# Two mixture layers with their routing rows broadcast by way of memory, in a transformer stack on one core

## The reference

```python
# layer 5, last part (8 experts): one expert per token
h = layernorm(x + attn_out, ln1_g, ln1_b)
_, top_i = top_k(softmax(h @ router_w.T + router_b), 2)
assign = max(top_i)                      # one expert number a token
for e in range(8):
    oe = gelu(h @ w1[e].T + b1[e]) @ w2[e].T + b2[e]
    out = where(assign == e, oe, out)
x += layernorm(h + out, ln2_g, ln2_b)
# layer 7 (16 experts, 4 chosen out of 2 of 4 groups, and a shared one)
scores = sigmoid(x @ gate_w.T);  s = scores + gate_bias   # s picks, scores weigh
comb[token, idx] = scores[token, idx]
y = einsum('tei,edi,te->td', silu(x @ w1) * (x @ w3), w2, comb)
z = silu(x @ ws1.T) * (x @ ws3.T) @ ws2.T
x += y + z
```

## Time and profile before

| | us |
|---|---|
| median of 3 runs (lowest, highest) | 1003.81 (1001.76, 1006.44) |
| the profiled execution, its own time | 1007.03 |
| its span on the core | 1005.2 |
| PE busy in the span | 730.2 |
| DVE busy in the span | 590.4 |
| ACT busy in the span | 355.2 |

### The profile page before, as it was taken

One profiled execution on the slowest core, in us unless ns is written; L12 is line 12 of the kernel. 1 busy time (PEld: TensorE's weight loads), 2 busy tenths in 40 slices (PEclk: granted clock), 3 DMA queues, 4 the chain that ended last, 5 costly groups with the idle time before them and its releaser, 6 DMA issues. The chain is left out here.

```text
span 1005.2 us, 13391 instructions
## 1 busy us (share of the span) xinstructions
PE 730.2 (73%) x3910; PEld 465.9 (46%) x3910; DVE 590.4 (59%) x2022; ACT 355.2 (35%) x634; POOL 251.8 (25%) x304
## 2 busy tenths in 40 slices
PE   2677762849839775588575757869886688699998
PEld 1233322848838621234364545556654233245554
DVE  6666644326305453775534564979887666576773
ACT  5355420624415332533332311212332466433231
POOL 2240466440343262512423321230210110000000
PEclk9999775869959767977896866989998899799999
DMA  6272022424524330215212100010220120000000
GB/s 175 56 269 74 24 86 69 120 89 116 152 66 130 101 100 19 76 48 204 61 49 80 49 6 1 1 71 2 62 61 17 32 71 25 0 1 11 11 11 11
DMA packets 71218, 65.55 MB, mean 65 GB/s; under 512 B 8996, under 2 KB 62941, under 8 KB 70634
## 3 DMA queue, kind: packets, MB, share of 16 engines
q1 hardware_dynamic: 53610, 48.02, 16.2%
q0 software_dynamic: 5120, 10.50, 3.5%
q10 hardware_dynamic: 12416, 6.16, 2.2%
HBM read 35.61 MB, written 22.94 MB: 58 GB/s over the span
## 5 line engine op out<-in xcount | busy, mean ns | idle before, releaser
L2540 POOL TENSOR_SCALAR s_vare<-s_mv 128x4 f32<-128x4 f32 x40 | 10.9, 272 | 433.8 <-DVE s_mv L1213 422.3
L1326 DVE TENSOR_REDUCE s_nmx<-psum_all 128x4 f32<-128x308 f32 x192 | 83.4, 473 | 56.8 <-PE psum_all L656 54.4
L2097 ACT ACTIVATE s_hT<-psum_all 77x1024 f32<-77x1024 f32 x96 | 96.0, 1017 | 57.2 <-PE psum_all L677 40.3
L675 PE MATMUL psum_all<-s_t,s_ks 128*77 128x512 bf16 x192 | 83.2, 434 | 10.5 <-ACT s_hT L2097 4.8
L656 PE MATMUL psum_all<-s_ks,s_t 128*128 128x308 bf16 x192 | 57.4, 348 | 40.4 <-DVE s_nmx L1326 25.5
L908 PE MATMUL psum_all<-s_arena,s_hT 128*128 x376 | 62.4, 300 | 32.1 <-issue 32.0
L677 PE MATMUL psum_all<-s_t,s_ks 128*77 128x512 bf16 x192 | 82.4, 429 | 0.0
L699 PE MATMUL psum_all<-s_hT,s_v 77*32 77x512 f32 x384 | 59.0, 688 | 32.2 <-ACT s_hT L2097 30.8
L2450 POOL DMA_INDIRECT s_w<-routed_y,s_cT x64 | 61.5, 961 | 69.6 <-issue 69.6
L2436 POOL DMA_INDIRECT routed_x<-s_x_normed,s_cT x64 | 62.5, 977 | 51.4 <-DVE s_cT L1527 33.1
L908 PEld LDWEIGHTS psum_all<-s_arena,s_hT 128*128 128x128 f32 x376 | 55.0, 204 | 36.1 <-issue 35.1
(11 more groups left out here) (311 smaller groups left out, 1555.1 us busy)
## 6 DMA issues: line engine op xcount, KB each, us to landing
s_t<-q_parts SPq DMA_DIRECT2D x66, 128.0 KB, 2.8
routed_y<-s_hT ACTq DMA_DIRECT2D x22, 256.0 KB
s_ks<-s_att SPq DMA_DIRECT2D x72, 77.0 KB, 2.1
q_parts<-s_qparts SPq DMA_DIRECT2D x11, 384.0 KB
s_arena<-in_w SPq DMA_DIRECT2D x2, 2048.0 KB, 10.3
s_h<-routed_x SPq DMA_DIRECT2D x48, 64.0 KB
s_x_normed<-routed_x SPq DMA_DIRECT2D x46, 64.0 KB
routed_x<-s_w SPq DMA_DIRECT2D x34, 64.0 KB
```

What stands on the lines that cost most here:

```text
L675: pe.matmul(PS[0:SK, k + y, :], KS1[:, h, keys], T1[:, u % QS, h // HPG, :], start=True, stop=False)
L1326: read(job, dve.tensor_reduce(nmx[:, u % 2, i, HPG * g:HPG * g + HPG], PS[:, k, 0:HPG * SK].rearrange("p (h s) -> p h s", h=HPG), AX.X, AL ...
L2097: read(("S", L, b, p), nc.scalar.activation(Eexp[:, (PAIRS * u + p) % ES, :, :], PS[0:SK, k:k + 2, :], ACT.Exp))
```

## The change

**Layer 7.** The bf16 split, `c7`, `pick7`, its load and the `CB` products go. PE turns the f32 weights (16 rows), ACT copies them to `cT`, SP writes them to memory (`CD`, 32 KB) and reads them back broadcast over partitions into two SBUF buffers of 1 MB each (`gates`: four pairs in each, 64 partitions for one expert). DVE multiplies the hidden rows by the buffer; the shared expert's pair is not multiplied. Routing runs two units ahead: batch 0 in (6, 2), batch 1 in (6, 3), batch 2 in (7, 0), batch 3 in (7, 1).

**Layer 5.** Batch 0 stays as it was. For batches 1 to 3 the one-hot choices (8 rows) go the same way (`CD5`, 16 KB, then two buffers of 1 MB, `choice`). DVE multiplies Gelu's output by the expert's broadcast row (one 128x512 instruction an expert), and PE sums the second bias and all eight experts in one ACC slot, which DVE adds once. PE makes hidden rows two experts ahead; result e waits for DVE's product e (`s_chosen`), and the stages of PE's step e come after hidden e+2. Batches 1 and 2 are routed in (5, 0), batch 3 in (5, 1), at the steps of `MHA_PLACES`.

**SP.** `spread_choices(1)`, `(2)` stand ahead of `place_k(2)`, `spread_choices(3)` behind it; `spread_gates(0)` behind `place_q(11)`, and each further one ahead of the wait for the output before it.

The core of the diff (`...` where it is cut):

```diff
-    5: {"front": (0, 0, 1), "R": (5, 5, 5), "CT": (7, 6, 7), "M0": (0, 0, 0), "M1": (1, 0, 0),
-        "M2": (2, 1, 0), "M3": (4, 3, 1), "MT": (4, 3, 6), "Q": (2, 3, 3), "stats+": (0, 3, 0),
+    5: {"M0": (0, 0, 0), "M1": (1, 1, 0),
+        "M2": (2, 2, 0), "M3": (4, 4, 1), "MT": (5, 5, 6), "Q": (2, 3, 3), "stats+": (0, 3, 0),
...
+MHA_PLACES = {
+    0: [((0, 0, 1), "front", 1), ((1, 1, 1), "R", 1), ((2, 2, 3), "CT", 1),
+        ((3, 0, 4), "front", 2), ((5, 5, 5), "R", 2), ((7, 6, 7), "CT", 2)],
+    1: [((0, 0, 1), "front", 3), ((3, 3, 3), "R", 3), ((6, 6, 6), "CT", 3)],
...
+            return (7, (b + 2) % NB) if (L, b) >= (6, 2) and (L, b) < (7, 2) else None
...
@@ PE, moe_unit
+                if b:
+                    hidden(1)
+                    have(("CT", L, b))
+                    k = start(("Y", L, b), ACC)
+                    for i in range(TPB):
+                        pe.matmul(PS[:, k, 128 * i:128 * i + 128], cT[0:E, b % 2, 128 * i:128 * i + 128],
+                                  b2[L][:, :], start=(i == 0), stop=False, skip_group_check=True)
+                    for e in range(E):
+                        pe.wait_ge(s_chosen, E * (b - 1) + e + 1)
+                        for i in range(TPB):
+                            mm = pe.matmul(PS[:, k, 128 * i:128 * i + 128], hT[:, (E * b + e) % HS, 0, 128 * i:128 * i + 128],
+                                           w2[L][:, e, 0, :], start=False, stop=(e == E - 1), skip_group_check=True)
+                        if e == E - 1:
+                            finish(("Y", L, b), mm)
+                        else:
+                            mm.then_inc(s_y5, 1)
+                        if e + 2 < E:
+                            hidden(e + 2)
+                        hook(e)
+                    return
...
@@ PE, glu_unit
-                    have(("CT", L, b))
-                    k = start(("CB", L, b, p), SMALL)
-                    finish(("CB", L, b, p), pe.matmul(PS[:, k, :], pick7[:, 128 * p:128 * p + 128],
-                                                      cT7[:, b % 2, :], start=True, stop=True))
...
-                    have(("CB", L, b, p))
+                    pe.wait_ge(s_gated, GLU_PAIRS * b + p + 1)
...
@@ DVE, route_glu
-                d = c7[:, b % 2, :, :]
-                link(dve.tensor_copy(c7h[:, 0, :, :], c))
-                dve.tensor_copy(d[:, :, 0:16], c7h[:, 0, :, :])
-                link(dve.tensor_tensor(lg[:, :, :], c, c7h[:, 0, :, :], ALU.subtract))
-                link(dve.tensor_copy(c7h[:, 1, :, :], lg[:, :, :]))
-                dve.tensor_copy(d[:, :, 16:32], c7h[:, 1, :, :])
-                dve.tensor_tensor(d[:, :, 32:48], lg[:, :, :], c7h[:, 1, :, :], ALU.subtract).then_inc(s_cw, 1)
...
@@ DVE, moe_unit
+                if b:
+                    for e in range(E):
+                        h = hT[:, (E * b + e) % HS, 0, :]
+                        dve.wait_ge(*slots.is_read(("H", L, b, e)))
+                        if e % 4 == 0:
+                            dve.wait_ge(s_choice[e // 4], 16 * b)
+                        dve.tensor_tensor(h, choice[b][e // 4][:, e % 4, :], h, ALU.mult).then_inc(s_chosen, 1)
+                        hook(e)
+                    k = made(("Y", L, b))
+                    last = ("Y", L, b)
+                    read(last, dve.tensor_tensor(d, PS[:, k, :].rearrange("p (i d) -> p i d", i=TPB), d, ALU.add))
...
@@ DVE, glu_unit
+                    if p < GATED:
+                        read(("H", L, b, p), dve.tensor_tensor(gl[:, x, 0, :], PS[:, k + 1, :], gl[:, x, 0, :], ALU.mult))
+                        settled(("H", L, b, p))
+                        if p % 4 == 0:
+                            dve.wait_ge(s_gate[p // 4], 32 * (b + 1))
+                        dve.tensor_tensor(gl[:, x, 1, :], gates[b % 2][p // 4][:, p % 4, :], gl[:, x, 0, :], ALU.mult).then_inc(s_gated, 1)
+                    else:
+                        read(("H", L, b, p), dve.tensor_tensor(gl[:, x, 1, :], PS[:, k + 1, :], gl[:, x, 0, :], ALU.mult))
+                        settled(("H", L, b, p))
+                        dve.sem_inc(s_gated, 1)
...
@@ ACT
-                    if step == 3 and (L, b) == (0, 0):
-                        act.wait_ge(s_rows, 16 * 4)
-                        nc.scalar.copy(pick7[:, :], H5[0:64, 0:GLU_PAIRS, :].rearrange("p a b -> p (a b)")).then_inc(s_pick, 1)
...
@@ SP
-            sp.dma_start(H5[0:64, 0:GLU_PAIRS, :], A["pick_pair"]).then_inc(s_rows, 16)
...
+            def spread_choices(b):
+                if b == 3:
+                    sp.wait_ge(s_chosen, EXPERTS[5])
+                sp.wait_ge(*slots.is_read(("CT", 5, b)))
+                sp.dma_start(CD5[b], cT[0:EXPERTS[5], b % 2, :]).then_inc(s_cd5, 16)
+                sp.wait_ge(s_cd5, 16 * b)
+                for x in range(2):
+                    if b > 1:
+                        sp.wait_ge(s_choice[x], 16 * (b - 1))
+                    sp.dma_start(choice[b][x], CD5[b][4 * x:4 * x + 4, :].partition_broadcast(P)).then_inc(s_choice[x], 16)
+            spread_choices(1)
+            spread_choices(2)
             place_k(2)
+            spread_choices(3)
+            def spread_gates(b):
+                if b >= 2:
+                    sp.wait_ge(s_gated, GLU_PAIRS * (b - 1))
+                sp.wait_ge(*slots.is_read(("CT", 7, b)))
+                sp.dma_start(CD[b], cT[0:EXPERTS[7], b % 2, :]).then_inc(s_cd, 16)
+                sp.wait_ge(s_cd, 16 * (b + 1))
+                by_half = CD[b].rearrange("(a p h) c -> a h p c", a=2, h=2)
+                for x in range(2):
+                    if b:
+                        sp.wait_ge(s_gate[x], 32 * b)
+                    for half in range(2):
+                        sp.dma_start(gates[b % 2][x][64 * half:64 * half + 64, :, :],
+                                     by_half[x, half].partition_broadcast(64)).then_inc(s_gate[x], 16)
```

More of the change, by code:

```diff
@@ L78 @@
              ((7, 6.5, 7), "MT", 2, 3)],
+}
+MHA_PLACES = {
[3 rows of a table added]
 }
@@ L422, in build @@
         s_sil = sem("silu_ready")
+        s_gated = sem("gated_rows_ready")
+        s_cd = sem("gates_stored")
+        s_gate = [sem(f"gates_loaded{x}") for x in range(2)]
         s_lg = sem("gauss_arg_ready")
@@ L518, in plan @@
                 todo += [("stats", *v), ("norm", *v)]
-            todo = [(PLACES[L][x[0] + "+" * (x[0] in ("stats", "norm", "front") and LAYERS[x[1]] == ATTN)][which], *x)
+            todo = [x if len(x) == 4 else
+                    (PLACES[L][x[0] + "+" * (x[0] in ("stats", "norm", "front") and LAYERS[x[1]] == ATTN)][which], *x)
                     for x in todo]
@@ L1462, in moe_unit @@
-                last = ("B2", L, b)
-                for e in range(E):
-                    k = made(("Y", L, b, e))
-                    settled(last)
-                    for i in range(TPB):
-                        t = TPB * b + i
-                        ins = dve.scalar_tensor_tensor(dst[:, t, :], PS[:, k, 128 * i:128 * i + 128],
-                                                       C[:, t, e:e + 1], dst[:, t, :], ALU.mult, ALU.add)
-                    last = ("Y", L, b, e)
-                    read(last, ins)
-                    hook(e)
@@ L1473, in moe_unit @@
-                settled(last)
-                if L == 5:
-                    x = tiles(X, b)
-                    norm_stats("ln2", L, b, d)
-                    link(dve.tensor_tensor(x, x, over(row("ln2_b"), TPB), ALU.add))
-                    link(norm_scaled("ln2", L, b, d, tiles(XN, b), row("ln2_g"), lambda i: X[:, TPB * b + i, :], x))
+                if b:
[9 more added lines that the diff above has]
+                    read(last, dve.tensor_tensor(d, PS[:, k, :].rearrange("p (i d) -> p i d", i=TPB), d, ALU.add))
+                else:
+                    k = made(("B2", L, b))
+                    read(("B2", L, b), dve.tensor_tensor(d, PS[:, k, :].rearrange("p (i d) -> p i d", i=TPB), d, ALU.add))
+                    last = ("B2", L, b)
+                    for e in range(E):
+                        k = made(("Y", L, b, e))
+                        settled(last)
+                        for i in range(TPB):
+                            t = TPB * b + i
+                            ins = dve.scalar_tensor_tensor(dst[:, t, :], PS[:, k, 128 * i:128 * i + 128],
+                                                           C[:, t, e:e + 1], dst[:, t, :], ALU.mult, ALU.add)
+                        last = ("Y", L, b, e)
+                        read(last, ins)
+                        hook(e)
@@ L1481, in small @@
+                settled(last)
+                x = tiles(X, b)
+                norm_stats("ln2", L, b, d)
+                link(dve.tensor_tensor(x, x, over(row("ln2_b"), TPB), ALU.add))
+                link(norm_scaled("ln2", L, b, d, tiles(XN, b), row("ln2_g"), lambda i: X[:, TPB * b + i, :], x))
             def small(t, a, n):
@@ L2716, in constants @@
```

(8 more changed lines are left out.)

97 lines of the change are left out of this document (53 added, 44 removed).

## The result

The changed kernel takes 1033.06 us in the median of 5 runs (1030.6 to 1041.71), the kernel before in the same set 1001.76 (996.52 to 1006.44). The ratio is 1.032, with a 95% interval from 1.029 to 1.035: 3.2% slower. I had forecast slower, by 6 us, with a range up to 1018. The direction was right, the size was five times too small. The profiled execution of the changed kernel took 1041.71 (span 1039.6), 8.7 us above its median.

What follows compares the result with a forecast made beforehand. PE was taken to bound layer 7 (97% busy in the last four units), PE and DVE waiting on each other layer 5. -19.1 - 1.2 - 1.5 + 9.5 + 18.3 = +6.0 on 1003.8 gave 1009.8 us, own range 1004 to 1018.

Steps and rivals of the forecast that it cites:

- Layer 5, the waits: Layer 5's four units: PE and DVE wait for each other, +5.1, +3.7, +2.9 and +1.2, together +12.9 us.
- the clock: Layer 5: PE runs slower after new idles; three counted at 1.8 us each, +5.4 us.
- My upper bound of 25 for the layer: Layer 5's high case: all five new idles cost slow clock, and 1.8 us twice more in (5, 3), +25.
- (6, 2): Layer 6's third unit takes over the routing of (7, 0): +9.5 us, range 4.3 to 12.
- the sum's four terms: In (6, 2): later `R` 2.5, late exponentials 2.8, wait before turned weights 3.4, PE's uncovered part 0.8 us.
- (6, 3): End of (6, 3): the bf16 split goes from the wait for the turned weights, -1.2 us.
- Layer 7: Spread off PE, 0.52 us a pair, and routing moved out: -2.2, -5.0, -7.3 and -4.6, together -19.1 us.
- The start: Program start: a load ahead of DVE's first scale and ACT's copy go, -1.5 us (0 to -2.7).
- Transfers at nothing: Row stores and loads in layers 5 and 7 cost 0; rival of late rows, +16 us, chance 0.05.
- The sign: Whole kernel: slower, by +6.0 us; chance of slower 0.48.
- PE stays fed in layer 5: Faster rival: DVE's hooks fit PE's time in layer 5, giving -4 there, -21.5 in all, 982.3 us; chance 0.15.
- one waiting line: Layer 5: result waits for product, product for DVE's other work ahead, which may wait for PE; argued against the faster rival.

Runs made afterwards that it cites:

- e4: The changed kernel plus 67 extra unread matmuls ahead of layer 5's waiting results and batch 1's turned choices; 1012.99 us, ratio 1.013.
- e10: e9 plus six extra matmuls ahead of the values' sum in each of (6, 2) and (6, 3); 980.78 us, ratio 0.981.
- e7: e1, but in (6, 2) and (6, 3) DVE does the routing's last piece ahead of the add waiting for PE; 909.83 us beside 924.66, ratio 0.982.
- e8: The kernel before, with gates by way of memory only for layer 7's batches 1 to 3, routed one unit ahead; 921.13 us beside 924.66, ratio 0.998.
- e9: The changed kernel, reordered: two products inside the layer norm, DVE's other work one product behind, batch 1's turned choices later, e7's order; 982.95 us, ratio 0.986.
- e1: The changed kernel with layer 5 as it was before; 996.52 us, ratio 0.9945.

## Why the prediction was wrong in size

**Layer 5, the waits: direction right, 12.9 forecast, 18.7 measured (e4).** By unit, at full clock, (5, 0) was laid out rightly (+5.3 for +5.1), as was (5, 2) (+3.3 for +2.9); (5, 1) was 2.5 us longer and (5, 3) 2.7. The waits stood where I put them: 3.22 us ahead of the first turned choices, 4.03 and 4.25 at the heads, 3.48 at step 4. What made the small misses up was not taken apart further.

**The step that failed: the clock, 5.4 forecast, 16.1 measured (20 by the medians).** I named five new idles of 3.4 to 4.3 us, wrote "I count three that cost 1.8" with no reason for leaving out the other two, and gave (5, 3) nothing, though I had laid out four experts there in which PE and DVE hand over to each other. The trace shows the slow pace behind each of the seven waits of over 3 us in layer 5, two of them in (5, 3); there, where short waits follow one another as well (0.39, 0.28, 1.17 us), the clock is 0.74 and costs 7.3 us. My upper bound of 25 for the layer had seven such stretches at 1.8 each and did not hold the 34.8 either: the waits themselves were 5.8 us longer than laid out, and the clock cost more than seven times 1.8. The Trainium skill (TensorE: Matmul & The Clock Gate, "HAM oscillation — how this bites in real kernels") describes this pattern: a kernel in which every wait between bursts, there for a transfer, puts PE back to the low clock, so that the price is paid at each and not once. The traces here agree for most waits: behind 4.03, 4.25 and 3.41 us a result of 1.05 takes 2.07, the pace of 1.2 GHz, and with matmuls in the waits the clock stays at 1.00, 2.4 GHz (e4, e10). They don't agree for all: of the twelve waits of over 1 us for a product or the turned choices in layer 5, nine have the slow pace behind them.

**(6, 2): +9.5 forecast, +11.5 measured.** Two of the sum's four terms can be seen as laid out: 3.19 us for the exponentials behind two table loads, 2.55 for the routing's last piece. The other two were not taken apart. e7 shows that the price is the wait and the slow clock behind it, and that the second was an order, not work.

**(6, 3): -1.2 forecast, +1.4 measured.** The split went: the wait for the turned weights is 2.56 (925.78) for 3.73 before. But the clock of the stretch is 0.69, for 0.78 before, with a wait at its head that before does not have; e7, without that wait, has 0.81.

**Layer 7: -19.1 forecast, -16.8 measured.** 0.52 us a pair, (7, 2), (7, 3) and (7, 0) were right to 0.3 us. In (7, 1) I missed a new wait of 0.90 and some 1.3 us that stay open.

**The start: -1.5 forecast, not to be told.** Executions of kernels that are alike up to layer 5, but for the load in question, reach it between 676 and 688 us in the sets with the slower start, and both profiled executions at 688.4.

**Transfers at nothing: right.** No product or pair waited for rows in the changed kernel; e8 shows how near that is.

**The sign.** Slower was the net of +27.8 and -21.8, six us, and layer 5 alone missed by over 16. That the sign came out right rests on the misses having mostly gone the same way, and is in part luck.

**The rivals.** "PE stays fed in layer 5" was false for this kernel and is what e9 comes close to: the work allows it, the order did not. I had weighed it against "one waiting line" as though both were given by the work.

## What to carry to other kernels

When an edit turns a running sum into "product, then result", lay out who stands ahead of the product on its engine, and put the product ahead of anything that waits for the other engine's same step. That was worth 32 us here, with no work removed. When a layout gives PE new waits such as these, charge the slow stretch behind most of them (nine of twelve here), not behind a few, and don't take a unit of many short waits for free. If such a wait can't be removed, matmuls that nobody reads, sized to the wait, give back part of it; try them first as a measurement of what the clock costs.

## What the runs showed of the hardware

- 67 extra matmuls made a kernel 20 us faster (e4): the waits of layer 5 cost nearly as much again in clock (16.1 us) as in length (18.7).
- With a wait of 2.56 us at its head and waits of 3.19 and 1.20 inside, unit (6, 3) has a clock of 0.69 over 27.5 us (e1); without the first wait it has 0.81 (e7), and with the 3.19 filled too 1.00 (e10).
- Not every wait did it: behind 1.97 us (743.62) and 2.48 us (761.60) in the changed kernel the next hidden products ran at full pace, and so did those behind one wait of 1.17 us (815.55), but not those behind another (797.27). The kernel before came out of a wait of 3.19 us at full pace, 1.06 us for eight matmuls, where the changed kernel's (6, 2) needs 1.94 behind the same wait. What decides between the two was not tried.

```profile
862.85 1.06 PE L699 MATMUL psum_all<-s_hT,s_v 77*32 77x512 f32 x8 [3.19 <-ACT s_hT L2097]
...
889.48 1.94 PE L743 MATMUL psum_all<-s_hT,s_v 77*32 77x512 f32 x8 [3.19 <-ACT s_hT L2156]
```

- A store of 16 rows and the load of the first half of their spread took 9.3 us from the store's start to first use (e8).
- The layers ahead of layer 5 took 73 us less in one set of runs than in another with the same code (e7, e1); what makes that was not tried.
- Between exponential, sigmoid and exponential, ACT's two table loads of 1.28 us each stand with nothing but the sigmoid's 0.22 between them, before and after (885.48 to 888.31).
